# A two-layer cross-attention kernel on one core: another order for the shift rows, value copies, transposed norm and a value share

## What is computed

```python
# layer 0: queries from x, keys and values from [ctx, x], 512 keys
q = (latents @ q_w + q_b).reshape(b, k_len, NH, DH)
kv = (h @ kv_w + kv_b).reshape(b, p + k_len, NH, DH, 2)
attn = jnp.einsum('bkhd,bnhd->bhkn', q, kmat) / DH
attn = jnp.where(full_mask[:, None, None, :], attn, -jnp.inf)
attn = jax.nn.softmax(attn.astype(jnp.float32), axis=-1).astype(q.dtype)
attn_out = attn_out @ out_w + out_b + residual
out = rmsnorm(attn_out, postnorm_w)
out = jax.nn.gelu(out @ mlp_w1 + mlp_b1) @ mlp_w2 + mlp_b2
return out + residual
# layer 1: queries from layer 0's result, keys and values from layer_norm(ctx), 256 keys
scores = jnp.einsum('bhtd,bhsd->bhts', Q, K) * scale
attn = jax.nn.softmax(scores, axis=-1)
out = out @ Wo.T
return hidden_states + jnp.tanh(gate) * out
```

## Time and profile before

| | |
|---|---|
| median of 3 runs | 2539.66 us (2539.37 to 2540.51) |
| profiled execution | 2538.97 us |
| its span | 2537.1 us |
| TensorE busy | 2357.6 us, 93% |
| ScalarE busy | 1477.8 us, 58% |
| VectorE busy | 1183.1 us, 47% |
| GpSimd busy | 231.4 us, 9% |
| TensorE's mean granted clock | 0.981 of full speed |
| transfers | 239.00 MB, mean 94 GB/s |

### The profile page before, as it was taken

The page is one execution under the profiler, slowest core; times in us unless marked ns, Lnnn a source line. Parts: engine busy times, 40 slices in busy tenths (PEclk is TensorE's granted clock), DMA queues, the critical chain, the costliest instruction groups (busy, mean ns, idle before and its releaser), DMA issues. The chain is left out here.

```text
span 2537.1 us, 43888 instructions
## 1 busy us (share of the span) xinstructions
PE 2357.6 (93%) x14656; PEld 1917.8 (76%) x14656; DVE 1183.1 (47%) x2350; ACT 1477.8 (58%) x3418; POOL 231.4 (9%) x260
## 2 busy tenths in 40 slices
PE   6899999999999999889999999999899898989897
PEld 4677777777777777668888888888687787878785
DVE  4455555555555555533122122112266565656564
ACT  3677777777777777753222222222266767676766
POOL 2000000000000000010000000000221111121210
PEclk9899999999999999989999999999899999999998
DMA  6244444444444443341111011012145454545442
GB/s 175 73 103 103 101 101 101 102 108 109 109 109 108 108 109 92 92 146 50 51 50 47 2 50 50 17 33 83 67 112 144 109 146 105 145 107 144 108 126 76
DMA packets 148186, 239.00 MB, mean 94 GB/s; under 512 B 25600, under 2 KB 59680, under 8 KB 148144
## 3 DMA queue, kind: packets, MB, share of 16 engines
q1 hardware_dynamic: 148144, 238.46, 35.3%
HBM read 86.28 MB, written 25.21 MB: 44 GB/s over the span
## 5 line engine op out<-in xcount | busy, mean ns | idle before, releaser
L534 ACT ACTIVATE l_score_ps<-l_score_ps,l_neg_max 128x512 f32<-128x512 f32 (+1 forms) x1024 | 569.1, 570 | 159.7 <-DVE l_neg_max L760 159.5
L760 DVE TENSOR_REDUCE l_neg_max<-l_score_ps 128x1 f32<-128x512 f32 (+1 forms) x768 | 490.4, 682 | 58.7 <-PE l_score_ps L1032 55.4
L554 ACT ACTIVATE l_probs<-l_score_ps 128x1024 f32<-128x1024 f32 x384 | 381.4, 1023 | 84.7 <-PE l_score_ps L1065 81.8
L1396 ACT ACTIVATE mlp_hidden<-mlp_hidden_ps,mlp_b_col 128x512 f32<-128x512 f32 x128 | 88.3, 690 | 496.3 <-PE mlp_hidden_ps L67 496.2
L1032 PE MATMUL l_score_ps<-l_stack 97*128 97x512 f32 (+1 forms) x1024 | 309.6, 368 | 54.1 <-ACT l_score_ps L534 40.5
L1431 DVE TENSOR_TENSOR mlp_hidden_l<-mlp_hidden,mlp_hidden_h 128x512 fp32r<-128x512 f32 x128 | 92.7, 724 | 519.6 <-ACT mlp_hidden_h L1398 519.6
L1065 PE MATMUL l_score_ps<-l_stack 99*128 99x256 f32 x1536 | 248.5, 294 | 22.2 <-DMA l_stack<-l_shiftT 21.3
L1065 PEld LDWEIGHTS l_score_ps<-l_stack 99*128 99x128 f32 x1536 | 212.9, 193 | 71.4 <-issue 25.1
L1032 PEld LDWEIGHTS l_score_ps<-l_stack 97*128 97x128 f32 x1024 | 175.1, 194 | 104.6 <-ACT l_score_ps L534 75.0
L534 ACT ACTIVATION_READ_ACCUMULATOR l_score_ps<-l_score_ps,l_neg_max 128x1 f32 x1024 | 227.7, 222 | 0.0
L65 PE MATMUL mlp_hidden_ps<-mlp_norm_h,mlp_w_l 128*128 128x512 f32 x512 | 200.3, 391 | 6.4 <-DVE mlp_norm_l L1426 6.4
(11 more groups left out here) (136 smaller groups left out, 4272.7 us busy)
## 6 DMA issues: line engine op xcount, KB each, us to landing
l_stack<-room SPq DMA_DIRECT2D x256, 192.0 KB
l_stack<-l_qk SPq DMA_DIRECT2D x256, 128.0 KB
l_stack<-room SPq DMA_DIRECT2D x128, 128.0 KB
l_stack<-l_qk SPq DMA_DIRECT2D x256, 64.0 KB
l_tokens<-in_x SPq DMA_DIRECT2D x16, 512.0 KB, 4.9
l_tokens<-in_ctx SPq DMA_DIRECT2D x16, 512.0 KB, 5.8
l_stack<-room SPq DMA_DIRECT2D x128, 64.0 KB
l_rows<-in_x SPq DMA_DIRECT2D x16, 512.0 KB, 3.4
```

The costliest lines, as they stand in the source:

```text
L534: m = act.activation(e, e, ACT.Exp, bias=neg_max[:, q, h:h + 1], accum_out=row_sum[:, q, h:h + 1])
L554: act.activation(probs[:, s % PROBS, :].rearrange("p (a b) -> p a b", a=2), score_ps[:, 2 * (s % 2):2 * (s % 2) + 2, :], ACT.Exp).then_inc ...
L760: dve.tensor_reduce(out, bank, AXIS_X, ALU.max, negate=True).then_inc(max_done, 1)
L1396: act.activation(hidden[:, m % HBUF, :], hidden_ps[m % 4][:, :], ACT.Gelu_apprx_tanh, bias=b1_col[:, m:m + 1])
```

## The change

In words, part by part:

- **Layer 0, slots.** `turn_shift(0)` moves from behind item 5 to behind item 4, with `make_shift(0)` and `copy_shift(0)`. `turn_norm` moves from behind item 4 to behind item 5, and waits for the copy of the shift. The wait for `nT_done` moves from `turn_shift` to `spread_sums(0)`, which stays behind item 6. Two steps come earlier in the first part.
- **Layer 0, values.** The copies of the two plain value blocks go from ScalarE to VectorE.
- **Layer 0, norm.** `weigh_norm` is cut in two halves of two operations each, which stand behind the maxima of steps 29 and 30, in item 6's slot. Before, all four stood at the start of item 5's slot, ahead of its first maximum.
- **Both layers.** `make_shift(1)` comes ahead of item 6's low part; `copy_inv(0)` goes behind the second exponential.
- **Layer 1.** Scores 0 and 1 go into the slot of the share, ahead of item 0, and the other steps move with them. `turn_shift(0)` comes behind item 4. `v_ahead` makes two shares instead of one, and stands ahead of the third projection instead of the fourth. SyncE loads tokens ahead of rows.

The diff:

```diff
--- before.py
+++ after.py
@@ -120,12 +120,13 @@
     RUN = 4
     AHEAD = RING if first else 0
 
-    STEPS_AT_FIRST = [0, 0, 4, 4, 4, 4, 4, 4, 4, 4] if first else [0, 0, 2, 2, 2, 3, 4, 3]
-    STEPS_IN_SLOT = [2, 4, 4, 1, 1, 1, 3, 4, 4, 4] if first else [0, 0, 2, 2, 2, 3, 3, 4]
+    STEPS_AT_FIRST = [0, 0, 4, 4, 4, 4, 4, 4, 4, 4] if first else [0, 0, 2, 3, 3, 3, 3, 2]
+    STEPS_IN_SLOT = [2, 4, 4, 2, 1, 2, 1, 4, 4, 4] if first else [2, 0, 2, 2, 2, 3, 3, 2]
     AFTER_T = SLOT.index(("item", NT))
-    TURN_SLOT = AFTER_T + 1
-    SPREAD_SLOT = TURN_SLOT + 1
-    SQUARE_SLOT, SCALE_SLOT, NORM_SLOT = 1, 3, AFTER_T
+    V_AHEAD = 1 if first else 2
+    TURN_SLOT = AFTER_T
+    SPREAD_SLOT = TURN_SLOT + 2
+    SQUARE_SLOT, SCALE_SLOT, NORM_SLOT = 1, 3, TURN_SLOT + 1
 
 
     assert max(STEPS_IN_SLOT + STEPS_AT_FIRST) <= RING
@@ -285,7 +286,7 @@
         def sums_later(slot):
 
             kind, n = SLOT[slot]
-            return kind == "item" and n < NT
+            return (kind == "item" and n < NT) or (kind == "share" and not first)
 
         def kind_of(slot, p, a):
 
@@ -360,10 +361,12 @@
             sp.wait_ge(const_made, CONSTS)
 
             def iteration(p, a, prev):
-                if a is not None:
-
+                def load_rows():
                     at_least(sp, norm_turned if first else stored, a if first else 16 * a)
                     sp.dma_start(rows[:, :, :], res_view[a]).then_inc(rows_loaded, 16)
+
+                if first and a is not None:
+                    load_rows()
                 if first and prev is not None:
                     sp.wait_ge(nT_done, prev + 1)
                     sp.dma_start(result[prev], nT[:, :, :]).then_inc(stored, 16)
@@ -371,6 +374,8 @@
 
                     sp.wait_ge(item_done, ITEMS * p + NT)
                     load_tokens(sp, p + 1)
+                if not first and a is not None:
+                    load_rows()
                 if a is not None:
                     for half in range(HALVES):
                         sp.wait_ge(shift_copied, HALVES * a + half + 1)
@@ -572,6 +577,7 @@
                 exps(a, 0)
                 copy_shift(a, 1)
                 exps(a, 1)
+                copy_inv(a, 0)
                 exps(a, 2)
                 copy_inv(a, 1)
                 exps(a, 3)
@@ -623,9 +630,7 @@
                 for slot in range(SLOTS + 1):
 
                     kind, n = kind_of(slot - 1, p, a)
-                    if kind == "v":
-                        copy_v(a, n)
-                    elif kind == "item" and n >= NT:
+                    if kind == "item" and n >= NT:
                         high(p, n)
 
                     kind, n = kind_of(slot, p, a)
@@ -634,8 +639,6 @@
                     if a is not None:
                         if TURN_SLOT == slot - 1:
                             copy_shift(a, 0)
-                        if SPREAD_SLOT == slot - 1:
-                            copy_inv(a, 0)
                         if first and slot == AFTER_T:
                             for t in range(PLAIN_V, KB):
                                 copy_v(a, t)
@@ -822,43 +825,51 @@
                     n = dve.tensor_scalar(rows[:, t, :], rows[:, t, :], stat[:, t, 2:3], None, ALU.mult)
                 n.then_inc(norm_done, 1)
 
-            def weigh_norm(b):
+            def weigh_norm(b, begin):
 
                 dve.wait_ge(norm_turned, b + 1)
-                for f in range(FB):
+                for f in range(begin, begin + GROUPS):
                     n = dve.tensor_scalar(nT[:, f, :], o_ps[f // 2][:, S * (f % 2):S * (f % 2 + 1)],
                                           post_w[:, f:f + 1], None, ALU.mult)
-                n.then_inc(nT_done, 1)
+                if begin + GROUPS == FB:
+                    n.then_inc(nT_done, 1)
+
+            def copy_v(b, t):
+
+                dve.wait_ge(v_done, KB * b + t + 1)
+                at_least(dve, pv_done, PSTEPS * b)
+                dve.tensor_copy(v[:, t, :], v_bank(t)).then_inc(v_copied, 1)
 
             def iteration(p, a, prev):
                 for slot in range(SLOTS + 1):
                     steps = steps_of(slot, a) if a is not None and slot < SLOTS else []
                     kind, n = kind_of(slot, p, a)
+                    for k in steps[:1]:
+                        step_max(a, k)
                     if kind == "item" and n < NT:
                         low(p, n)
-                    if first and prev is not None and slot == NORM_SLOT + 1:
-                        weigh_norm(prev)
-                    for k in steps[:1]:
-                        step_max(a, k)
                     if a is not None and TURN_SLOT == slot:
                         make_shift(a, 0)
+                    if a is not None and slot == SLOTS:
+                        make_shift(a, 1)
                     kind, n = kind_of(slot - 1, p, a)
                     if kind == "item" and n >= NT:
                         low(p, n)
                     if not first and a is not None and slot == AFTER_T:
                         for t in range(KB):
-                            dve.wait_ge(v_done, KB * a + t + 1)
-                            at_least(dve, pv_done, PSTEPS * a)
-                            dve.tensor_copy(v[:, t, :], v_bank(t)).then_inc(v_copied, 1)
+                            copy_v(a, t)
                     for k in steps[1:]:
                         step_max(a, k)
+                        if first and prev is not None and slot == NORM_SLOT + 1 and k < steps[-1]:
+                            weigh_norm(prev, (k - steps[1]) * GROUPS)
+                    if kind_of(slot, p, a)[0] == "v":
+                        copy_v(a, SLOT[slot][1])
                     if first and prev is not None:
                         if slot == SQUARE_SLOT:
                             square_rows(prev)
                         if slot == SCALE_SLOT:
                             scale_rows(prev)
                 norm_next = not first and p is not None and not (isinstance(p, int) and p == B - 1)
-                make_shift(a, 1)
                 if first:
                     if p is not None:
                         low(p, MIXED)
@@ -917,7 +928,8 @@
             if first:
                 square_rows(B - 1)
                 scale_rows(B - 1)
-                weigh_norm(B - 1)
+                for f in range(0, FB, GROUPS):
+                    weigh_norm(B - 1, f)
 
 
         @block.tensor
@@ -998,7 +1010,8 @@
 
                 pe.wait_ge(low_done, ITEMS * (b + 1))
                 pe.wait_ge(o_norm_done, FB * b - 1)
-                v_passes(b, PLAIN_V, 0)
+                for f in range(V_AHEAD):
+                    v_passes(b, PLAIN_V, f)
 
             def v_share(b, f):
 
@@ -1008,7 +1021,7 @@
                         pe.wait_ge(low_done, ITEMS)
                     at_least(pe, o_norm_done, FB * b)
                 for t in range(PLAIN_V, KB):
-                    if f == 0 and t == PLAIN_V and not at_first:
+                    if f < V_AHEAD and t == PLAIN_V and not at_first:
                         continue
                     n = v_passes(b, t, f)
                     if f == FB - 1:
@@ -1036,8 +1049,6 @@
             def turn_shift(a, half):
                 pe.wait_ge(shift_made, HALVES * a + half + 1)
                 pe.wait_ge(v_copied, KB * (a + 1))
-                if first:
-                    at_least(pe, nT_done, a)
                 at_least(pe, o_norm_done, FB * a)
                 for q in range(QT):
                     n = pe.transpose(o_ps[half][0:SHIFT_ROWS, P * q:P * (q + 1)], shift[:, half, q, :], ident[:, :])
@@ -1046,6 +1057,8 @@
             def spread_sums(a, half):
 
                 pe.wait_ge(shift_copied, HALVES * a + half + 1)
+                if first and half == 0:
+                    at_least(pe, nT_done, a)
                 for g in range(GROUPS):
                     n = pe.matmul(o_ps[half][:, S * g:S * (g + 1)], spread[:, g, :], shiftT[:, half, :],
                                   start=True, stop=True)
@@ -1117,6 +1130,8 @@
                 shifted(a, 7)
                 project(a, 1)
                 run(1)
+                if p is not None:
+                    v_ahead(p)
                 project(a, 2)
 
             def second_pass_of_four_keys(p, a, run):
@@ -1180,6 +1196,7 @@
                     if a is not None and SLOT[slot][0] == "item" and 1 <= n < FB - 1:
                         v_share(a, n + 1)
                     if first and prev is not None and slot == NORM_SLOT:
+                        pe.wait_ge(shift_copied, HALVES * a + 1)
                         turn_norm(prev)
                     if a is not None and TURN_SLOT == slot:
                         turn_shift(a, 0)
@@ -1212,8 +1229,6 @@
                     second_pass_of_four_keys(p, a, run)
                 else:
                     second_pass_of_two_keys(p, a, run)
-                if p is not None:
-                    v_ahead(p)
                 project(a, 3)
 
```

## The result

The changed kernel takes 2622.51 us (median of 4 runs, 2618.23 to 2626.29) against 2539.51 for the kernel before: a ratio of 1.0327, 95% interval 1.0307 to 1.0346. It is 83 us slower; 2652 was predicted, with a range from 2575 to 2680.

What follows compares the result with a forecast made beforehand. TensorE was taken as busy for most of the span, so time comes from or goes into its idle stretches. 2538.97 us + 94 for layer 0 + 19 for layer 1 = 2652, range 2,575 to 2,680.

Steps and rivals of the forecast that it cites:

- store issue at 19 after item 0: Layer 0, profile after: sign that SyncE issues the store 19 us after the turn's item 0, shift rows right behind the tokens.
- taken as gained up to item 4's end: Layer 0, TensorE: of 1.4 us a turn waited for sums, 0.9 goes, so item 4 ends at 282.1, not 283.02.
- Predicted at 291.5: Layer 0, VectorE: nT_done comes at 291.5, 5.8 us later, its halves standing behind the maxima of steps 29 and 30.
- held by the tokens: Layer 0, SyncE's queue: shift rows wait behind the tokens, so shifted(0) starts at 298.8 against 294.09, +4.7 us a turn.
- the shift rows overtake the tokens: Rival, layer 0 queue: shifted(0) at 296.3, 2.5 us a turn less than forecast, some 2,617 in all; chance 0.10.
- the 2.6 taken: Layer 0, TensorE's clock: falls behind the wait for shift rows in each turn, costing 2.6 us a turn.
- digits under 9 all along both loops: Sign in the profile after: TensorE's clock digits read under 9 throughout both layers' loops.
- if the digits stay at 9: Both loops: the prediction counts as wrong if TensorE's clock digits stay at 9 in the profile after.
- S + 25.1 for score 8: Layer 1: SyncE's full queue lets score 8 start no earlier than 25.1 us after shifted(3) starts.
- Idle was put at 3.1: Layer 1: TensorE, ready at S + 21.8 to 22.2, waits about 3.1 us a turn for score 8's stack.
- the fall was put down for each turn at 2.1: Layer 1: the clock falls behind score 8's wait, costing 2.1 us a turn, +29 for 14 turns.
- layer 1 keeps its clock: Rival, layer 1: no clock fall, so -10 us there and 2,623 in all; chance 0.18, shared with its stack in time.

Runs made afterwards that it cites:

- e11: Kernel with shift rows first, weighing behind step 28's maximum, four stack semaphores in layer 1; layer 0's two plain value copies back on ScalarE: 2486.26 us, 0.9793.
- e4: Changed kernel, but in layer 0 SyncE writes the first half's shift rows behind rows, nT_done and store, ahead of the tokens: 2580.0 us, 1.0164.
- e3: Changed kernel, but in layer 0 SyncE writes the first half's shift rows ahead of rows, nT_done, store and tokens: 2511.96 us, 0.9896.
- e2: The change in layer 1 only, with layer 0 as in the kernel before: 2541.75 us, 1.0008.
- e10: Kernel before, with only SyncE's layer 0 order altered: first half's shift rows ahead of rows, nT_done, store and tokens: 2590.15 us, 1.0212.
- e6: On e3, layer 1's half-stack pieces count on four semaphores, one per head of a group, so score 8 needs only five transfers: 2494.42 us, 0.9822.

## Why the prediction was right, step by step

The result lies in the range, 30 under the forecast: some 10 of this are layer 0's (84 for 94) and some 17 layer 1's (2 for 19).

**The first part of a turn.** The row at 272.26, which the forecast called item 0, is item 1; item 0 stands at 270.62. The times of the forecast don't hang on it, only the sign "store issue at 19 after item 0", which from the true item 0 is 21 and came at 21.3. 0.9 was taken as gained up to item 4's end; it is 1.1 (12.40 to 11.28 from item 0). Of this, 0.4 is the wait for the value copy, which I left at 0.8 and which fell to 0.4, so 0.7 is left for the sums. e11 shows that the copies' move carries little of this once the rest is in place; which of the moves gave the rest was not tried apart.

**`nT_done`.** Predicted at 291.5, or item 0 + 20.9; it came at + 21.0. The two maxima and item 6 hold it, as said.

**SyncE's queue and the tokens.** `shifted(0)` was predicted at 298.8, item 0 + 28.2; it came at 27.9. The choice between "held by the tokens" and "overtakes" is settled by e4: 2.84 from issue without them, 4.73 with them. The Trainium skill's rule in "DMA: Bandwidth & Descriptors", section "Queues, rings and completion order", that an engine takes a ring's descriptors in order, agrees with this. The load that the tokens put on the engines would look the same here, and no run takes the two apart. The rival "the shift rows overtake the tokens" named a total of 2,617, near the measured one, but by a path that the trace rules out. e3 shows that it is this order that makes the difference between 28 faster and 83 slower.

**The clock in layer 0.** It falls in each of the 13 turns of the loop, and costs 2.4 against the 2.6 taken. With the second `shift`'s wait gone and 0.3 less at `shifted(0)`, these terms give +6.2 a turn; it is +6.0 instead of +6.7: 84 instead of 94. One sign was badly set: "digits under 9 all along both loops", with the forecast wrong "if the digits stay at 9". They stay at 9 throughout layer 0's loop, although the clock falls in each turn, because 5.1 us at half clock in a turn of 71.7 leave a mean of 0.96. By its letter the sign spoke against the forecast; the windows behind `shifted(0)` are what shows the falls.

**Layer 1** is where the sum was off: +19 predicted, about +2 measured (e2). S + 25.1 for score 8 (S is the start of `shifted(3)`) was right (2232.57 to 2257.76 is 25.19), and the turn without a fall, 41.4 predicted, is 41.1. Two terms were mis-sized. Idle was put at 3.1 and is 2.2 to 2.4 from the third turn on: TensorE came to score 8 later than I worked out, S + 22.8 instead of 21.8 to 22.2. And the fall was put down for each turn at 2.1. It comes in 7 of the 13 turns between the first item 0 of the loop and its last: in both that wait 3.5 to 3.75, about as long as the wait of 3.33 from which the forecast took it, but in only 5 of the 11 that wait 2.2 to 2.4. In four of these 5 it costs 1.4 (42.5 against 41.1), in one 2.7, where the clock stayed down longer (a mean of 0.60 instead of 0.79 in the 8 us from score 8). The mean turn is 42.3. The rival "layer 1 keeps its clock" (2,623) hits the total, but half of the turns don't keep it. The Trainium skill tells in "TensorE: Matmul & The Clock Gate", section "HAM oscillation — how this bites in real kernels", of a loop in which a wait for a transfer of about 3 to 5 us brings the clock down in every turn. Layer 0 of the change agrees (waits of 5.4 to 6.1, a fall behind each). Layer 1's waits of 2.2 to 2.4 are shorter than the Trainium skill's, and still brought it down in 5 of 11 turns.

**The forecast's blind spot** did no harm here but would have in e10: `copy_inv(0)` waits for the store to land. Its move has no term in my sum, and I gave no reason for that. Nor did I see that layer 1's turn of 41.1 is held by sums and the value copies as much as by SyncE: both limits give nearly the same time, and only e6 took them apart.

## What to carry to other kernels

To make a small result early is worth nothing if the queue that carries it stands at an older wait: move the transfer together with the work, and look at what its place in the queue is behind. Here the same work order was 83 us slower or 28 faster by the place of one pair of 8 KB transfers. When a wait goes away and the time doesn't, compare the turn with an undisturbed one: in e6 the wait for the stack was only the visible end of slack that another chain sets.

## What the hardware showed that I had not expected

A wait of about 2.3 us in each turn of layer 1 brings TensorE's clock down in 5 of 11 turns (6 of 11 in e2), with nothing in the program different between them: turns of 41.1 and 42.5 stand side by side. In e4 a wait of 2.2, with another of 1.3 shortly ahead of it, brings it down each time, and turns still vary from 67.6 to 68.7, since it isn't down equally long (0.68 and 0.79 over 8 us). And a transfer of 8 KB behind a store of 512 KB took no longer than in an idle queue (2.84 and 2.82), while behind 1 MB of loads it took 4.73. The store itself lands 2.7 after its issue in e4 and so ahead of `shifted(0)`, so this doesn't show that a store holds nothing, only that one of this size costs nothing here.
